# A graph kernel's first edge product turned round: one-hots stationary, weighted rows with the weight as last column moving, two masked additions per group, and no separate weight sums

## What is computed

```python
h = (feat - mean) * rsqrt(var + EPS) * gamma + beta
feat_in, feat_out = h @ W_in + b_in, h @ W_out + b_out
a_in  = segment_sum(feat_in[src] * iw[:, None], dst)
a_out = segment_sum(feat_out[dst] * ow[:, None], src)
xi = concatenate((a_in, a_out), axis=1) @ W_x2i + b_x2i
...                                # gates, layernorm(x + layer)
support = segment_sum(edge_weight[:, None] * feature[src], dst)
output = support @ weight + bias   # layernorm(x + layer) again
```

## Time and profile before

| | |
|---|---|
| three runs | 3967.5, 3975.3 (median), 3986.6 us |
| the profiled execution | 3983.0 us, its span 3981.2 us |
| granted TensorE clock, mean | 0.816 of full |
| busy share of the span | PE 67%, weight loads 48%, DVE 58%, ACT 27%, POOL 65% |
| DMA | 142 GB/s mean, 245 GB/s from 1.8 to 2.5 ms |

### The profile page before, as it was taken

The page is one execution under the profiler, slowest core; times in us unless marked ns, Lnnn a source line. Parts: engine busy times, 40 slices in busy tenths (PEclk is TensorE's granted clock), DMA queues, the critical chain, the costliest instruction groups (busy, mean ns, idle before and its releaser), DMA issues.

```text
span 3981.2 us, 47940 instructions
## 1 busy us (share of the span) xinstructions
PE 2656.6 (67%) x10701; PEld 1905.5 (48%) x10701; DVE 2302.5 (58%) x4510; ACT 1059.2 (27%) x3137; POOL 2607.6 (65%) x2706
## 2 busy tenths in 40 slices
PE   4666766566666566648888888996656545545467
PEld 4455543333333333337777777643434334333356
DVE  6866866566565565645666666686335445444355
ACT  3233322222222222224444444463000000000012
POOL 5666666666666666665666666476667777777764
PEclk8777777777787877779999999998777777777688
DMA  5443343333343333347878887554333333333333
GB/s 149 138 130 106 95 139 130 130 133 132 128 140 131 134 130 130 128 150 236 248 246 244 249 245 245 182 166 137 90 90 93 93 94 91 91 93 93 91 115 97
DMA packets 275042, 565.31 MB, mean 142 GB/s; under 512 B 55583, under 2 KB 121110, under 8 KB 274771
## 3 DMA queue, kind: packets, MB, share of 16 engines
q0 software_dynamic: 119808, 329.02, 26.5%
q1 hardware_dynamic: 146304, 223.88, 18.3%
q10 hardware_dynamic: 8660, 9.41, 0.7%
HBM read 419.19 MB, written 142.88 MB: 141 GB/s over the span
## 4 chain that ended last, share of the span: by engine, by line
PE 34%; another core or an unknown queue 26%; issue 17%; DVE 11%; POOL 7%; ACT 2%; DMA 1%; DVEq 1%; SPq 1%; ACTq 0%; POOLq 0%
PE ps L1140 10%; PE ps L952 8%; POOL messages L547 6%; PE ps L1211 5%; PE ps L1072 3%; PE ps L1101 2%; PE ps L1173 2%; PE ps L1258 1%; ACT arena L729 1%; DVE arena L1758 1%; POOL arena L541 1%; DVE ps L1582 1%; DVE arena L1761 1%; PE ps L1087 1%
## 5 line engine op out<-in xcount | busy, mean ns | idle before, releaser
L547 POOL DMA_INDIRECT messages<-arena x832 | 830.1, 998 | 428.8 <-issue 239.2
L541 POOL DMA_INDIRECT arena<-in_x,arena x832 | 792.7, 953 | 471.1 <-issue 209.2
L619 POOL DMA_INDIRECT arena<-x_table,wh x832 | 841.4, 1011 | 365.8 <-issue 241.8
L1211 PE MATMUL ps<-arena 128*128 x2048 | 597.0, 443 | 385.5 <-issue 134.7
L1211 PEld LDWEIGHTS ps<-arena 128*128 128x128 f32 x2048 | 438.1, 222 | 549.4 <-issue 487.3
L952 PE MATMUL ps<-arena 128*128 128x128 f32 x3328 | 490.5, 309 | 238.6 <-issue 168.4
L952 PEld LDWEIGHTS ps<-arena 128*128 128x128 f32 x3328 | 462.3, 221 | 319.6 <-issue 270.9
L729 ACT ACTIVATE arena<-ps,arena 128x256 f32<-128x256 f32 x832 | 325.1, 481 | 910.3 <-remote 435.0
L1072 PE MATMUL ps<-arena 128*128 128x256 f32 x1664 | 489.8, 447 | 10.7 <-issue 5.2
L2174 DVE TENSOR_TENSOR node_a<-node_a,ps 128x256 f32 x256 | 106.8, 417 | 637.3 <-remote 453.9
L1072 PEld LDWEIGHTS ps<-arena 128*128 128x128 f32 x1664 | 381.8, 231 | 104.2 <-issue 38.2
(11 more groups left out here) (280 smaller groups left out, 3374.9 us busy)
## 6 DMA issues: line engine op xcount, KB each, us to landing
arena<-messages SPq DMA_DIRECT2D x464, 260.0 KB
arena<-in_x SPq DMA_DIRECT2D x304, 128.0 KB, 2.9
gate_rows<-arena SPq DMA_DIRECT2D x49, 384.0 KB
arena<-gate_rows SPq DMA_DIRECT2D x49, 384.0 KB, 3.0
arena<-in_x,arena POOLq DMA_INDIRECT x832
messages<-arena POOLq DMA_INDIRECT x832
arena<-x_table,wh POOLq DMA_INDIRECT x832
arena<-in_x SPq DMA_DIRECT2D x48, 256.0 KB
```

Source lines behind the costliest of these rows:

```text
L541: nc.gpsimd.indirect_dma_start(out=big[:, s, j, 0:D], out_offset=None, in_=x, in_offset=bass.IndirectOffsetOnAxis(ap=ids[:, j:j + 1], axis ...
L547: nc.gpsimd.indirect_dma_start(out=messages, out_offset=bass.IndirectOffsetOnAxis(ap=ids[:, j:j + 1], axis=0), in_=big[:, s, j, :], in_off ...
L619: nc.gpsimd.indirect_dma_start(out=last_rows[:, (g + 1) % LAST_ROWS, j * D:(j + 1) * D], out_offset=None, in_=x1_table, in_offset=bass.Ind ...
L1211: last = nc.tensor.matmul(ps[g % LAST_SUMS][:, 0:D], last_hot[h][:, j, :], last_rows[:, bass.ds(k, 1), j * D:(j + 1) * D].rearrange("p o d ...
```

## The change

The product is turned round. The one-hot of a group's places is now the stationary operand and the rows move; the place is dst modulo 128, so the sum comes out with nodes on the partitions. The rows carry the weight as column 256, so the moving operand has 257 columns and the sum of weights falls out as the last column. A group's destinations can lie in two neighbouring node tiles, so DVE adds the sum twice, to tile t under a mask of the partitions from the group's first place on, and to tile t+1 under the mask of the rest. `node_a` becomes 257 wide with nodes on the partitions. The one-hots of weights, their sum, the row on partition 0 and its way through HBM are removed. In the gates stage the a_in sums are now transposed as well. The zeroing of `node_c` is spread over ten turns of the second stage.

```diff
+AW = D + 1
...
-        node_a = sb("node_a", [P, NTP, D])
+        node_a = sb("node_a", [P, NTP, AW])
...
+            sp.wait_ge(S["weights_turned"], 4)
+            sp.dma_start(lows_b, row_view(group_row).broadcast_to([P, NG])).then_inc(S["low_rows"], 16)
...
-            sp.wait_ge(S["w_summed"], 1)
-            sp.dma_start(row_view(weight_row), in_w_row[:, 0:NT * P]).then_inc(S["row_kept"], 16)
...
                 act.wait_ge(S[f"in_rows{s}"], (i + 1) * 16 * CPG)
+                nc.scalar.activation(big[:, s, :, D:AW], carried[:, bass.ds((RING * i + s) * CPG, CPG), 1:2], ACT.Copy)
...
-                    nc.scalar.activation(node_rows[:, s, :], tile_of(node_c, t), ACT.Copy).then_inc(S["e_rows"], 1)
+                    nc.scalar.activation(node_rows[:, s, 0:D], tile_of(node_a, t), ACT.Copy)
+                    nc.scalar.activation(node_rows[:, s, D:2 * D], tile_of(node_c, t), ACT.Copy).then_inc(S["e_rows"], 1)
...
-                    nc.scalar.activation(st[:, r, 0:2, :], in_sums[:, :, bass.ds((t - 1) * P, P)], ACT.Copy)
                     act.wait_ge(S["e_turned"], t)
-                    nc.scalar.activation(st[:, r, 2:4, :], halves(ps[r][:, 0:D]), ACT.Copy).then_inc(S["e_out"], 1)
+                    nc.scalar.activation(st[:, r, :, :], ps[r][:, :].rearrange("p (k n) -> p k n", k=4), ACT.Copy).then_inc(S["e_out"], 1)
...
-                need(pe, S["in_added"], g - 1)
-                for k in range(2):
-                    for j in range(CPG):
-                        last = nc.tensor.matmul(ps[4 + h][:, k * P:(k + 1) * P], big[:, s, j, k * P:(k + 1) * P],
-                                                hot[:, h, j, :], start=j == 0, stop=j == CPG - 1)
+                need(pe, S["in_added"], 2 * (g - 1))
+                for j in range(CPG):
+                    last = nc.tensor.matmul(ps[4 + h][:, 0:AW], hot[:, h, j, :], big[:, s, j, 0:AW], start=j == 0, stop=j == CPG - 1)
...
-                    if s % 2:
-                        pe.wait_ge(S["w_hot"], g + 1)
-                        need(pe, S["w_added"], g - 1)
-                        if s == 1 and tiles:
-                            pe.wait_ge(S["c_out"], i + 1)
-                        nc.tensor.matmul(ps[4][0:1, 0:2 * P], ones[:, 0:1], weighed.rearrange("p k n -> p (k n)"),
-                                         start=True, stop=True).then_inc(S["w_mm"], 2)
                     if s == 0 and tiles:
                         pe.wait_ge(S["cx_loaded"], (i + 1) * 16)
                         need(pe, S["c_out"], i)
-                        need(pe, S["w_added"], g)
...
                 dve.wait_ge(S["in_mm"], g + 1)
-                need(dve, S["in_added"], g)
-                o = in_sums[:, :, bass.ds(low, P)]
-                V.tensor_tensor(o, o, halves(ps[4 + s % 2][:, 0:D]), ALU.add).then_inc(S["in_added"], 1)
+                need(dve, S["in_added"], 2 * g)
+                for k, mask_of in ((0, low_mask), (1, high_mask)):
+                    m = carried[:, bass.ds(g, 1), 2 + k] if kept else mask_of[:, bass.ds(g, 1)]
+                    o = tile_of(node_a, tile + k, AW)
+                    V.scalar_tensor_tensor(o, ps[4 + s % 2][:, 0:AW], m, o, ALU.mult, ALU.add).then_inc(S["in_added"], 1)
...
-                V.tensor_tensor(hot_w[:, h, :, :], numbers.rearrange("p (o n) -> p o n", o=1).broadcast_to([P, CPG, P]),
-                                place[:, bass.ds(g * CPG, CPG)].rearrange("p (c o) -> p c o", o=1).broadcast_to([P, CPG, P]),
-                                ALU.is_equal).then_inc(S["w_chain"], 1)
...
-                V.tensor_tensor(hot_w[:, h, :, :], hot_w[:, h, :, :], carried[:, bass.ds(g * CPG, CPG), 1:2].broadcast_to([P, CPG, P]),
-                                ALU.mult).then_inc(S["w_chain"], 1)
...
-                V.tensor_reduce(weighed[:, h, :], hot_w[:, h, :, :].rearrange("p j n -> p n j"), AX.X, ALU.add).then_inc(S["w_hot"], 1)
...
+                if NT - CLEARS <= i:
+                    n = i - NT + CLEARS
+                    V.memset(node_c[:, n * NTP // CLEARS:(n + 1) * NTP // CLEARS, :], 0.0).then_inc(S["sums_zeroed"], 1)
```

More of the change, by code:

```diff
@@ L938, in _ @@
                 turn(ps[4 + n % 2], raw[2 + n // 2], n % 2, S["weights_turned"])
-            pe.wait_ge(S["lows"], 1)
-            for n in range(2, 6):
+            for n in range(2, 4):
                 pe.wait_ge(S["columns_copied"], n - 1)
-                turn(ps[6 + n % 2], (raw_place, raw[1])[n // 2 - 1], n % 2, S["columns_turned"])
+                turn(ps[6 + n % 2], raw[1], n % 2, S["columns_turned"])
             def in_mm(i, s):
@@ L1520, in hot_in, with windows, low_tiles, add_in @@
                                 ALU.is_equal).then_inc(S["in_hot"], 1)
-            def two_lows(i, s):
-                v = V.value_load(low_two[0:1, bass.ds(2 * i + s // 2, 1)]).with_bounds(min_val=0, max_val=((N - P) << LOW_BITS) + N - P)
-                return [(v & ((1 << LOW_BITS) - 1)).with_bounds(min_val=0, max_val=N - P),
-                        (v >> LOW_BITS).with_bounds(min_val=0, max_val=N - P)]
-            def add_in(g, s, low):
-                dve.wait_ge(S["in_mm"], g + 1)
-                need(dve, S["in_added"], g)
-                o = in_sums[:, :, bass.ds(low, P)]
-                V.tensor_tensor(o, o, halves(ps[4 + s % 2][:, 0:D]), ALU.add).then_inc(S["in_added"], 1)
-            def in_turn(i, beside=(), first=False, last=False, between=None, numbers=numbers_in):
+            def windows(n, of, table, most=NT):
+                v = V.value_load(table[0:1, bass.ds(n, 1)]).with_bounds(min_val=0, max_val=1 << (4 * WIN_BITS))
+                return [((v >> (WIN_BITS * u)) & ((1 << WIN_BITS) - 1)).with_bounds(min_val=0, max_val=most) for u in of]
+            def low_tiles(i, of=range(RING)):
+                return windows(i, of, low_four, (N - P) // P)
+            def add_in(g, s, tile, kept=False):
+                dve.wait_ge(S["in_mm"], g + 1)
+                need(dve, S["in_added"], 2 * g)
[3 more added lines that the diff above has]
+                    V.scalar_tensor_tensor(o, ps[4 + s % 2][:, 0:AW], m, o, ALU.mult, ALU.add).then_inc(S["in_added"], 1)
+            def in_turn(i, beside=(), first=False, last=False, between=None, numbers=numbers_in, held=None, kept=False):
+                tiles = held
                 for s in range(RING):
@@ L1541, in in_turn @@
                         step()
-                    if s == 0 and not first:
-                        lows = two_lows(i - 1, 2)
-                    elif s % 2:
-                        lows = two_lows(i, s - 1)
-                    if not (first and s == 0):
-                        add_in(g - 1, (s - 1) % RING, lows[(s - 1) % 2])
+                    if s == 0 and not first and not held:
+                        add_in(g - 1, RING - 1, low_tiles(i - 1, [RING - 1])[0], kept)
+                    elif s == 0 and not first:
+                        add_in(g - 1, RING - 1, held[RING - 1], kept)
+                    elif s == 1:
+                        tiles = low_tiles(i)
+                    if s:
+                        add_in(g - 1, s - 1, tiles[s - 1], kept)
+                    if s or not first:
                         if staged_turn(i) and not (last and s > 0):
@@ L1554, in in_turn @@
                         between()
+                return tiles
             def staged_turn(i):
@@ L1720, in _ @@
             for i in range(RANKED, FIRST - 1):
-                in_turn(i, in_order([step for n in range(BASES_T) for step in base_steps((i - RANKED) * BASES_T + n)]), between=prep.get(i))
+                held = in_turn(i, in_order([step for n in range(BASES_T) for step in base_steps((i - RANKED) * BASES_T + n)]),
+                               between=prep.get(i), held=held)
             def turn_slots(link, a, r, m, h):
```

196 lines of the change are left out of this document (80 added, 116 removed).

## The result

The changed kernel took 3998.2 us (median of 7 runs, 3990.7 to 3999.7), the kernel before 3975.1 (7 runs): a ratio of 1.0055, interval 1.0041 to 1.0068. The forecast was 3750 us, 0.94.

What follows compares the result with a forecast made beforehand. No engine was taken as full: the weight-sum ring held POOL in the second stage, weight loads held PE in the third. From 3983.0 us, 5 - 140 - 3 - 100 + 10 = -228 gave 3755, less 8, taken as 3750; range 3670 to 3900.

Steps and rivals of the forecast that it cites:

- Short matmuls are held by their loads: Third stage, first product on PE: each of 16 short records waits for a 201 ns weight load, 3.2 us a group.
- The check that 3.2 + 3.25 us is about the period of 6.12: Third stage, PE: loads of 3.2 us plus back products of 3.25 give 6.45 us, so PE can be full.
- rival A: Third stage gains nothing on PE, columns being equal; the second addition lengthens the ring: +54 us, about 3900; chance 0.2.
- The prediction's own sign: Third stage: time from product start to release near 3.5 us; staying near 4.8 would make the reading of loads wrong.
- Third stage, -100: 128 groups: fewer loads save 1.4 us, the second addition costs 0.42; period 6.12 to 5.35 us, -100 us.
- Second stage, -140: Removing the weight sums from the ring saves 2.85 us in each of 49 turns, -140 us; bounds -187.5 and 0.
- together up to 3.8 us, against 3.76 us of wait: Second stage, per turn: weight products (2.0 us) and the way to the transposes (1.8) leave the ring; POOL waits 3.76.
- The ring through the weight sums: Second stage: PE's weight product and the transposes behind DVE's weight-sum addition hold the turn at 24.41 us.
- POOL's floor: POOL's own work as the next bound: 20.95 us a turn in the second stage, 5.01 us a group in the third.
- First stage, +5: 80 groups: a second DVE addition of 0.42 us each, less removed work; +5 us, bounds +34 and -60.
- Gates, +10: Gates stage, 49 tiles: two more transposes on PE cost 0.22 us a tile, +10 us.
- Rival C: Product releases lag by a fixed latency, so POOL waits on and both second additions lie on rings: +98, 4081 us; chance 0.05.

Runs made afterwards that it cites:

- e3: The changed kernel with its first product cut into 128 and 129 columns, so 16 short records and weight loads a group again: 1.0017 of the kernel before.
- e6: The kernel before, unedited, profiled again on a chip without late releases, where it takes 3519 us; second stage 1084.8 us, third 677.1.
- e1: The changed kernel without its second masked addition: 0.9918 of the kernel before, third stage 667.6 us.
- e4: The changed kernel with the next group's `hot_in` ahead of the two additions in the third stage: 0.994 of the kernel before, third stage 663.2 us.
- e2: The kernel before without any work on weight sums in the second stage: 0.9913 of the kernel before, on a chip without late releases.
- f2: The kernel before without any work on weight sums in the second stage, once more: 0.9929 of the kernel before, without late releases.
- e5: The changed kernel, unedited, on a chip without late releases: 3516.5 us, 1.0022 of the kernel before.
- e8: The changed kernel with 258 columns and the next group's `hot_in` ahead of the two additions in the third stage: 3493.7 us, 0.996 of the kernel before.

## Why the prediction was wrong

It forecast -228 us and the other sign came. Two steps of its sum failed: the second stage's wait was put down to the weight sums, and the third stage's time from start to release to the weight loads. The measured changes there are -19.1 and +18.9 us, for -140 and -100. Point by point:

- **"Short matmuls are held by their loads"**: wrong where releases are not late. e3 put the 16 loads back and the stage stayed at 688 us; e6's step with 16 records is 5.27 us. So loads of 201 ns do not hold these matmuls by themselves; what splitting the product would do among late releases was not run. The check that 3.2 + 3.25 us is about the period of 6.12 was a coincidence. The earlier trace rows had what spoke against it, which rival A named: the starts are 112 ns apart. The 4.83 us from start to release hold a delay of about the same size in nearly every group (median 2.82 us behind the modelled end, half of them 2.1 to 2.9; 1.31 in e6), read as a cost of the work. The prediction's own sign, 3.5 us after the change, was nearly met (3.69), and yet the stage grew: the sign could not tell.
- **Third stage, -100**: the ordinary step did become 5.36, but without late releases it gains nothing from the product's form, with them no run shows that it does, and 22 late steps took it back: +18.9. Without late releases it is +11.8. Rival A had the mechanism (equal columns, the addition lengthens the ring) and +54 as its size. The addition was mis-sized from below, 0.48 for 0.42 us, and its share on the ring from above: 21 us for the second alone (e1), 26 for both (e4).
- **Second stage, -140**: wrong step "together up to 3.8 us, against 3.76 us of wait". The ring through the weight sums was there in order, but did not set when the results came: e6 has all of it and 19.8 us of wait, e2 and f2 have none of it and 12.9 and 9.8. The wait stayed (190.5 us), and the 19 to 25 us that the stage gained are shorter scatters, a term that the sum did not have, although hold scatters of 1.14 and 1.15 us beside one of 0.96.
- **POOL's floor**: I took 20.95 us a turn from one turn with its long scatters. e5's whole stage is 1059.5/52 = 20.4 us a turn.
- **First stage, +5**: -1.5 in the runs of the result, +5.5 without late releases. **Gates, +10**: +7.1 and +7.0; two transposes cost 0.14 us a tile, not 0.22. **Last stage, 0**: +2.2 and +5.0, unexplained.
- **Rival C** had the right sign and in kind the right mechanism for the second stage: a lag of its own that keeps POOL's wait. It decided from the second stage giving back under 98 us, and it gave 19. Its price, both additions in full (+98), was four times too high. Its chance of 0.05 was far too low: ACT's 8.30 us behind a record of 3.32 was a lag that nothing in the sum explained, and the sum was built on its going away. The lag itself is not fixed as C had it: it varies within a stage and from chip to chip.

## What to carry to other kernels

Where results come later than their records end, by more than the work explains, find out what the lag is before counting on a step that removes work ahead of it. A wait that ends with such a result is no measure of what the work in front of it costs. Look too whether engines that wait for nothing are slow in the same moments: that tells a delay of one engine's results from one that several share. Compare the same kernel on a second chip if one is to be had: here POOL's wait of 187.5 us was 19.8 on another. An addition that takes a result out of PSUM belongs behind the operation that the next product waits for: with `hot_in` ahead of the two additions the changed kernel is at 0.994 of the kernel before where releases are not late (1.0019 where they are). It and e8, the same with an even width, are the only versions here that compute all and are clearly faster anywhere; the kernel before in this order was not run on such a chip. None beats both kernels on both kinds of chip.

## What was not expected of the hardware

- Two kinds of chips: 3507 to 3519 and 3975 to 4023 us (medians) for the same kernel, with equal lengths of single operations (gathers 952 and 953 ns, additions 418 and 420), and the difference in waits alone.
- The third stage with late releases takes 824 us for 822 when 0.43 us a group of PE's work is added, and gets longer (846) when half of the first product is taken away.
- In late releases of the changed kernel ACT's register instructions, which wait for nothing, start 0.7 us apart instead of 0.02.
- A DVE multiplication with both operands in SBUF lengthens a scatter that starts during it from 0.96 to as much as 1.49 us.
- The masked addition from PSUM takes 480 ns at 257 and at 258 columns, where one of 256 with another mask operand took 425.
